# Moving the residual row transfers of a two-layer graph kernel from GpSimd to ScalarE and SyncE, and its layer-norm statistics one chunk later

## The reference

```python
h = jnp.maximum(_layernorm(x, axis=-1), 0.0)
x = x + _L0_gnn_ref(h, adj, L0_gnn_weight, L0_gnn_bias)     # x1 in the kernel
h = jnp.maximum(_layernorm(x, axis=-1), 0.0)                # h2 in the kernel
x = x + _L1_gnn_ref(h, L1_gnn_context, adj, ...)            # attention over adj > 0
```

## Time and profile before

| | |
|---|---|
| median of three runs | 557.08 us (556.97 to 557.21) |
| the profiled execution | 554.63 us, of which the span is 552.8 us |
| PE busy | 480.3 us (87%) |
| DVE busy | 447.1 us (81%) |
| ACT busy | 314.0 us (57%) |
| POOL busy | 271.7 us (49%) |
| mean TensorE clock granted over the span | 0.965 of full speed |

### The profile page before, as it was taken

How to read it: one execution, slowest core, us unless ns; L and a number is a source line. 1 busy time by engine, 2 the same in 40 slices (tenths; PEclk the granted TensorE clock), 3 DMA queues, 4 the chain that set the end, 5 groups by cost and what they waited for, 6 DMA issues and landing times.

```text
span 552.8 us, 9390 instructions
## 1 busy us (share of the span) xinstructions
PE 480.3 (87%) x3209; PEld 413.2 (75%) x3209; DVE 447.1 (81%) x907; ACT 314.0 (57%) x466; POOL 271.7 (49%) x348
## 2 busy tenths in 40 slices
PE   1733879999999999999994777899999999999995
PEld 1622758877787788888883556788888888888884
DVE  3997878777787798888888899968788787878763
ACT  1584767748586778686866632535353535353521
POOL 6840899999999675535357996202020202020200
PEclk9985999999999999999997879999999999999998
DMA  7899999999999999998970000110101010101010
GB/s 171 186 234 223 252 300 301 275 280 266 311 289 320 260 332 320 338 293 218 273 194 20 22 18 28 32 40 20 39 18 41 13 46 8 52 2 38 1 39 20
DMA packets 91851, 84.75 MB, mean 153 GB/s; under 512 B 7552, under 2 KB 89728, under 8 KB 91808
## 3 DMA queue, kind: packets, MB, share of 16 engines
q1 hardware_dynamic: 56032, 48.64, 35.4%
q10 hardware_dynamic: 33424, 31.20, 20.5%
q0 software_dynamic: 2352, 4.35, 2.9%
HBM read 79.96 MB, written 4.21 MB: 152 GB/s over the span
## 4 chain that ended last, share of the span: by engine, by line
PE 54%; POOL 24%; DVE 7%; SPq 7%; issue 3%; DMA 3%; ACT 2%; ACTq 0%; POOLq 0%; DVEq 0%
PE ps L749 35%; PE ps L716 19%; POOL mask L501 8%; POOL mask L492 7%; SPq L382 3%; SPq L299 2%; DVE room L1234 2%; DMA mask<-in_L_gnn_context_dram 2%; DVE room L1201 2%; SPq L373 2%; DVE room L1185 1%; POOL out_dram L589 1%; POOL post L559 1%; POOL xk L596 1%; DVE room L1208 1%
## 5 line engine op out<-in xcount | busy, mean ns | idle before, releaser
L716 PE MATMUL ps<-room 128*128 128x256 f32 x1024 | 227.9, 382 | 28.5 <-DVE room L1117 22.7
L749 PE MATMUL ps<-room 128*128 128x258 f16 x2048 | 232.3, 276 | 20.5 <-POOL room L629 15.0
L749 PEld LDWEIGHTS ps<-room 128*128 128x128 fp8e4 x2048 | 200.5, 98 | 52.3 <-issue 16.0
L716 PEld LDWEIGHTS ps<-room 128*128 128x128 f32 x1024 | 193.4, 191 | 60.6 <-DVE room L999 27.5
L871 ACT ACTIVATE mask<-room,constants 128x1024 int8<-128x1024 f32 x128 | 146.1, 1145 | 59.0 <-DVE room L999 56.3
L999 DVE STREAM_TRANSPOSE room<-room 128x512 f32<-128x512 f32 x184 | 124.5, 697 | 19.8 <-PE ps L716 11.2
L643 POOL TENSOR_TENSOR h_room<-h_room 128x512 f32<-128x512 f32 x7 | 8.9, 1275 | 146.3 <-DVE post L1275 146.3
L1201 DVE SCALAR_TENSOR_TENSOR room<-mask,constants,room 128x512 int32<-128x512 int32 x64 | 64.5, 1007 | 10.8 <-ACT room L919 10.8
L919 ACT ACTIVATE room<-relu_u,r_col 128x512 int8<-128x512 f32 x64 | 42.0, 713 | 40.6 <-PE ps L749 40.6
L919 ACT ACTIVATE room<-room,r_col 128x512 int8<-128x512 f32 x62 | 40.9, 712 | 34.5 <-PE ps L749 34.5
L999 DVE STREAM_TRANSPOSE room<-mask 128x512 f32<-128x512 f32 x72 | 48.9, 697 | 8.6 <-PE ps L716 4.2
(11 more groups left out here) (160 smaller groups left out, 343.1 us busy)
## 6 DMA issues: line engine op xcount, KB each, us to landing
room<-in_adj_dram SPq DMA_DIRECT2D x100, 256.0 KB, 7.6
room<-in_adj_dram ACTq DMA_DIRECT2D x84, 256.0 KB, 8.3
mask<-in_adj_dram SPq DMA_DIRECT2D x40, 256.0 KB, 8.1
mask<-in_adj_dram ACTq DMA_DIRECT2D x32, 256.0 KB, 9.0
mask<-in_L_gnn_context_dram SPq DMA_DIRECT2D x16, 256.0 KB, 11.7
xk<-in_x_dram POOLq DMA_DIRECT2D x32, 64.0 KB, 6.4
out_dram<-xk POOLq DMA_DIRECT2D x32, 64.0 KB, 4.8
h_room<-out_dram SPq DMA_DIRECT2D x32, 64.0 KB, 2.4
```

The costliest lines, as they stand in the source:

```text
L716: mm = pe.matmul(acc[parity][:, h], xt[:, tangent_order.index(blocks_of(c, k)[j]), :], turned[:, k % TSLOTS, j * (CH // 2):(j + 1) * (CH / ...
L749: mm = pe.matmul(ps[:, 2 * t + w, 0:GW], part[slot(c, g)][:, kk, t * P:(t + 1) * P], G[w][:, k, :], start=(k == 0), stop=(k == NK - 1))
```

## The change

Three things change.

1. POOL issues none of the transfers of `xk` any more. ACT stores x1 of chunk c - 2 after half 1 of chunk c, and loads the next rows of `x` right behind `normed` (in `normed_and_next`), where the issue waits for `x1_stored` and for ACT's own `h2_ready`. The first load stands at ACT's start. SP stores x1 of the last chunk.
2. `normed` moves from half 2 to half 5 of chunk c, and DVE's `spread` and `variance` of chunk c - 2 stand behind blocks 3, 4 and 5 of chunk c. Before, those of c - 1 stood behind blocks 28, 29 and 30. (For the second last chunk they still do.)
3. On POOL both remaining `beside` portions of a chunk come ahead of `affine`.

```diff
             sp.wait_ge(x1_ready, NC)
+            for b in range(NQ):
+                sp.dma_start(out_n[NC - 1, b], xk[b * Q:(b + 1) * Q]).then_inc(x1_stored, 16)
             neg_left_row(1, 1)
...
-            load_x(0)
             pool.wait_ge(v_copied, 1)
...
                 residual(p)
-                store_x1(p)
                 beside(BESIDE_FIRST + 3 * p + 1)
+                beside(BESIDE_FIRST + 3 * p + 2)
                 affine(p)
-                beside(BESIDE_FIRST + 3 * p + 2)
-                load_x(p + 1)
...
+            for b in range(NQ):
+                act.dma_start(xk[b * Q:(b + 1) * Q], x_n[0, b]).then_inc(xk_loaded, 16)
...
-                return copy, squares, tanh, normed
+
+                def store_x1():
+                    act.wait_ge(x1_ready, p + 1)
+                    for b in range(NQ):
+                        act.dma_start(out_n[p, b], xk[b * Q:(b + 1) * Q]).then_inc(x1_stored, 16)
+
+                def normed_and_next():
+                    normed()
+                    if p < NC - 1:
+                        act.wait_ge(x1_stored, (p + 1) * (16 * NQ))
+                        act.wait_ge(h2_ready, p + 1)
+                        for b in range(NQ):
+                            act.dma_start(xk[b * Q:(b + 1) * Q], x_n[p + 1, b]).then_inc(xk_loaded, 16)
+                return copy, squares, tanh, normed_and_next, store_x1
...
                 if c >= 2:
-                    steps[2] = post_steps(c - 2)[3]
+                    steps[1] = post_steps(c - 2)[4]
+                    steps[5] = post_steps(c - 2)[3]
+                if c == NC - 1:
+                    steps[15] = post_steps(c - 1)[4]
...
-                steps = {} if number and c == 0 else post_steps(c - 1)
+                steps = {}
+                if c >= 1:
+                    steps.update(zip((7, 12, 13), post_steps(c - 1)[0]))
+                if c >= 2:
+                    steps.update(zip((3, 4, 5), post_steps(c - 2)[1]))
+                if c == NC - 1:
+                    steps.update(zip((28, 29, 30), post_steps(c - 1)[1]))
```

More of the change, by code:

```diff
@@ L584, in _ @@
             POOL_POST = 9
-            def store_x1(p):
-                pool.wait_ge(x1_ready, p + 1)
-                for b in range(NQ):
-                    pool.dma_start(out_n[p, b], xk[b * Q:(b + 1) * Q]).then_inc(x1_stored, 16)
-            def load_x(p):
-                if p:
-                    pool.wait_ge(x1_stored, p * (16 * NQ))
-                    pool.wait_ge(h2_ready, p)
-                for b in range(NQ):
-                    pool.dma_start(xk[b * Q:(b + 1) * Q], x_n[p, b]).then_inc(xk_loaded, 16)
-            load_x(0)
             pool.wait_ge(v_copied, 1)
@@ L633, in _ @@
                     residual(NC - 1)
-                    store_x1(NC - 1)
                 if g == 4:
@@ L859, in signs @@
                 if c >= 1:
-                    copy, squares, tanh, _ = post_steps(c - 1)
+                    copy, squares, tanh, _, _ = post_steps(c - 1)
                     steps = {0: copy, 4: squares, 9: tanh}
                 if c >= 2:
-                    steps[2] = post_steps(c - 2)[3]
+                    steps[1] = post_steps(c - 2)[4]
+                    steps[5] = post_steps(c - 2)[3]
+                if c == NC - 1:
+                    steps[15] = post_steps(c - 1)[4]
                 if c == NC - 2:
@@ L892, in _ @@
             acc_of[0] = acc[1]
-            last_copy, last_squares, last_tanh, last_normed = post_steps(NC - 1)
+            last_copy, last_squares, last_tanh, last_normed, _ = post_steps(NC - 1)
             last_copy()
@@ L1153, in variance @@
                     ins.then_inc(var_ready, 1)
-                return {7: relu, 12: sums_u, 13: sums_relu, 28: lambda: spread((0, 1)), 29: lambda: spread((2, 3)),
-                        30: variance}
+                return [relu, sums_u, sums_relu], [lambda: spread((0, 1)), lambda: spread((2, 3)), variance]
             def turn(c, parity):
                 number = isinstance(c, int)
-                steps = {} if number and c == 0 else post_steps(c - 1)
+                steps = {}
[5 more added lines that the diff above has]
+                    steps.update(zip((28, 29, 30), post_steps(c - 1)[1]))
                 for k in range(NK):
@@ L1178, in _ @@
                 turn(c, c % 2)
-            last = [f for _, f in sorted(post_steps(NC - 1).items())]
+            last = [f for part in post_steps(NC - 1) for f in part]
             def compare(c, parity, g):
```

## The result

The changed kernel takes **575.89 us** (median of four runs, 571.08 to 578.32) against 557.03 for the kernel before, timed beside it (four runs, 556.6 to 557.21). The ratio is 1.035, 95% interval 1.031 to 1.038: **slower, by 19 us where 4 were forecast**, and outside the range. The profiled execution is 578.32 us for a span of 576.5. A run over 1.5% above the fastest of its kernel is left out of the ratios in this document: two of e5's ten, one of e8's six, and three of e7's four.

The account below looks back on a forecast made before the run. POOL was taken to pace chunks 1 to 4 and PE chunks 5 to 7; -8.2 + 13.0 - 1.0 = +3.8 us on 557.08 gave 560.9 us, with a range of 552.5 to 566.

Parts of the forecast that it names:

- direction, mechanism, place: Chunks 2 to 7: ACT's loads behind `normed` delay half 6's signs, PE stops at block 16; total 3.8 us slower.
- 1.0 forecast: Chunk 2: `affine` ends at 125.7 but ACT wants it at 124.7, so 1.0 us more is lost.
- The transition: Between phases 1 and 2: POOL earlier, ACT's loads later, between -2.7 and +0.5 us, taken as -1.0.
- the place called critical: Transition, L1201 at 310.18: 2.7 us sooner by POOL's path, 0.5 us worse by DVE's own.
- The rival in which nobody is held up: The load's wait holds nobody up, or the allowance is larger: 548 us with no stall; chance 0.23.
- The gain of 8.2: Phase 1: taking 5.1 us a chunk from POOL removes the gaps of chunks 1 to 4, 8.2 us.
- the loss of 13.0: Phase 1: PE stalls of 2.0 us in six chunks plus 1.0 more in chunk 2, 13.0 us.
- I take 2.0, in each of the chunks 2 to 7: PE at block 16 stands for 1.9 us, taken as 2.0, since ACT's loads delay the signs of half 6.
- The wait for `x1_stored` should not bind: ACT's load behind half 5: stores are issued 10 us before it, and big adj loads land in 8.3 us.
- The issue at 0.43 us: ACT's transfers: a pair of issues costs 0.87 us, the four loads 1.7, the tile's pair 0.9.
- The row with a pair at 1.99: ACT's earlier issue pair of 1.99 us; four extra issues at twice the price add 1.7 us per chunk, the upper end.
- The rival of the clogged queue: ACT's queue: issues take twice as long or `x1_stored` comes late, 1 to 1.5 us more in six chunks; chance 0.12.

Follow-up runs that it names:

- e5: Changed kernel with stores behind half 14 of the chunk before, two loads behind half 6 and two behind half 8, on ACT: 563.8 us, 1.0117.
- e8: The kernel of e1 with `normed` behind half 7 instead of half 5: 569.06 us, 1.0225.
- e7: Changed kernel with all phase 1 transfers of `xk` issued by SP: 554.22, 564.07, 569.95 and 575.38 us, no ratio.
- e3: Changed kernel with ACT's stores behind half 14 of the chunk before instead of half 1, loads unmoved: 570.66 us, 1.0278.
- e6: Kernel before with only the transfers moved to ACT: stores behind half 14 of the chunk before, loads behind `normed` at half 2: 562.28 us, 1.0099.
- e9: Changed kernel with ACT issuing only the two HIGH loads behind `normed`, POOL the two LOW ones behind `affine`: 566.49 us, 1.0219.
- e10: Kernel before plus four unused copies of rows of `x` to spare DRAM, issued by ACT behind half 5, waiting for nothing: 561.11 us, 1.0087.
- e1: Changed kernel with the loads of `xk` back on POOL behind `affine`, stores still on ACT: 553.84 us, 0.9978.
- e11: The kernel of e8 with POOL's loads behind `shrink` of the next chunk: 551.0 us, 0.9897.
- e2: Changed kernel with two loads behind half 6 and two behind half 8, still on ACT: 558.25 us, 1.0024.
- e4: Kernel before with statistics at blocks 3 to 5, `normed` at half 5, `affine` behind both portions, transfers still on POOL: 557.89 us, 1.0045.

## Why the prediction was wrong

**Right: direction, mechanism, place.** Chunk 1 at 28.07; no wait of DVE's statistics for POOL; one stop a chunk at block 16, through ACT, DVE and PE; `normed` 1.02 us late in chunk 2 behind `affine(0)`, against 1.0 forecast. The transition came out at -2.4 against -1.0, inside its bounds. POOL's first group of G begins 2.0 us behind PE's L689 instead of 4.3, and L1201, the place called critical (L1210 now), comes after 15.9 us instead of 17.7. The two instructions of L1185 (L1194 now) that took 2.44 us take 0.87 in the same place of the order, as the prediction supposed; DVE is busy for 53.45 us of the transition instead of 55.19. The -2.4 is nearer to the -2.7 that goes with the Trainium skill's rule on the shared port (SBUF — State Buffer, SBUF: two separate sides), a rule that the Trainium skill limits to certain kinds of DVE operations; no run tells the port's part from that of POOL's path. The signs written behind the loads never began before the loads were out, in the changed kernel, e3, e6 and e9, nor before the copies in e10. That agrees with the Trainium skill's rule on the sequencer (Perfetto Trace Analysis, DMA Instruction — HWDGE). The rival in which nobody is held up falls with e1, which gives it only when ACT does not load.

**The gain of 8.2**: DVE's waits for POOL were gone as forecast, and the stop took their place. e11 shows how much of it can be had: phase 1 from chunk 1 on in 198.7 us (91.24 to 289.96), 4.4 less than before, since a few short waits remain and the last chunk is longer (27.9 against 26.3).

**Wrong: the loss of 13.0**, measured at 32.5 in the profiled execution. The step that failed is the size of the stop, "I take 2.0, in each of the chunks 2 to 7". Three terms of it:
- "The wait for `x1_stored` should not bind": it bound in the chunks 3 to 5, by 1.8, 1.5 and 0.7 us. The prediction set 10 us against the 8.3 that a large load takes to land, but that is a median, and here all four stores have to land: the slowest took 10.0 to 10.9 us. Without this wait the same six stops come to 18.0 us (e3), so it stands for some 3.5 of the 21.5.
- The issue at 0.43 us: four took 1.77 to 2.67 us instead of 1.7, the pair behind them 0.95 to 2.08 instead of 0.9. The row with a pair at 1.99 was read as the exception and moved to the upper end; behind four loads the pair took 1.64 to 2.08 in three of the six chunks, and 1.23 to 2.06 in all six of e3. e10 shows dear issues without any wait, in the chunks 2 and 3. These dear issues are the larger part: e3's 18.0 us against the 13.0 forecast.
- The clock: no term at all. 8.1 us in the profiled execution, a quarter of the loss. The prediction counted PE's stop as the price of the stop.

The rival of the clogged queue named two of the three, priced them together at 1 to 1.5 us a chunk and gave them 0.12. Stops 8.5 us longer in all than the 13.0 forecast are 1.4 a chunk, inside that; with the clock it is 2.8.

**What stays open.** Which of two things makes an issue dear: ACT's queue being full, or the 16 DMA engines being busy. The queues' part of the changed kernel's page (packets, MB, share of the 16 engines' span; q10 is ACT's, q0 POOL's):

```profile
q10 hardware_dynamic: 42064, 35.14, 25.7%
q0 software_dynamic: 304, 0.15, 0.1%
```

The same of the kernel before:

```profile
q10 hardware_dynamic: 33424, 31.20, 20.5%
q0 software_dynamic: 2352, 4.35, 2.9%
```

The rows of `xk` were 2,048 packets of some 2 KB on POOL's queue; on ACT's queue 3.94 MB come with 8,640 packets, some 460 bytes each. The time of POOL's packets was 15 us of all 16 engines (2.8% of 552.8), and that of ACT's queue grew by 35 us (25.7% of 576.5 less 20.5% of 552.8). Not all of this growth need be the rows of `xk`: SP's queue, which carries 0.27 MB more, also takes 12 us more (36.1% of 576.5, 35.4% of 552.8). In phase 1 the engines are full in both kernels (a share of 1.03 or more), so this speaks for the second, but no run separated the two; e1 takes the loads out of ACT's queue and makes their packets large again at once. Also open is e5 against e2: in the profiled executions e5's phase 1 from chunk 1 on is 1 us shorter than e2's (208.2 and 209.3), and its span is 3.8 us longer behind phase 1, where their orders are the same. So are the spread of e7 and, in e6, what the place at half 5 costs.

## What to carry to other kernels

A DMA issue that waits for something its own engine has just made holds back all that stands behind it: give it a place where the engine has nothing urgent next, and behind everything that others wait for (e11 against e8 is only that). Price an issue by the longest row of its kind, not by the usual one, when the queue already carries a steady stream, and count all transfers that a wait needs, not one. If the bound engine is PE, a stop can cost more than its length: look at the granted clock behind a stop that the trace already has.

## What the runs showed of the hardware

The clock behind a stop of PE: 0.50 and 0.52 for some 3 us, or 1.5 to 1.7 us lost. The length of the stop alone did not decide it. It fell behind 1.92 us (e9, chunk 7: 0.64 in the 2.6 us behind it, 8.86 us for 32 records that take 7.17 else), 2.18 us (e10) and 2.56 us (e1), but not behind 3.35 us (e4, 16.67 us for 76 records) or 2.94 us (e9, chunk 6).

The same four issues of one instruction took 1.77 us in one chunk and 2.98 in another (chunks 6 of the changed kernel and 3 of e3), and three of the copies 1.92 and 3.46 in one run (e10).

A transfer of 64 KB on ACT's queue, with a steady stream of 256 KB transfers beside it, was long in landing: 6.3 us in the median of the 28 stores, 10.9 at most. A wait for four of them meets the slow one: in the chunks 2 to 5 the slowest took 10.0 to 10.9 us.

The same rows moved by POOL's queue and by ACT's queue were packets of different size, 2 KB and about 0.5 KB (2,048 packets for 4.2 MB, 8,640 for 3.94), with nothing changed in how the transfer is written.
